# A two-layer decoder on one core: weights split during the experts, operands carried on chip into the second scan, and a rewritten last stage

## The reference

```python
x = _layernorm(x + ssm0(x));  x = _layernorm(x + long_conv(ctx, ctx, x))
x = _layernorm(x + moe0(x))       # 64 experts, the 8 best per token, 128 places each
x = _layernorm(x + ssm1(x));  x = _layernorm(x + linear_attention(x, ctx))
x = _layernorm(x + moe1(x))       # 4 experts, the 2 best per token, 512 tokens each

# moe0, the end: each token sums the outputs of its slots
slot_out = yb[dest] * topk_w.reshape(-1)[:, None]
out = jnp.zeros((T, h), yb.dtype).at[slot_token].add(slot_out)

# ssm1: d_inner 1024, 16 states, rank 128
xs, z = jnp.split(x @ W_in.T, 2, axis=-1)
u = silu(conv4(xs) + conv_b)               # over 4 tokens, channel by channel
dt_r, Bm, Cm = split(u @ W_x.T, [128, 16, 16])
dt = jax.nn.softplus(dt_r @ W_dt.T + b_dt)
A = -jnp.exp(A_log)
h_t = exp(dt_t * A) * h_(t-1) + dt_t * B_t * u_t
y_t = sum over the 16 states of h_t * C_t, + u_t * D
return (y * silu(z)) @ W_out.T
```

## Time and profile before

| what | value |
|---|---|
| median of 3 runs | 4858.97 us (4854.84 to 4861.33) |
| the profiled execution | 4852.57 us |
| its span, first to last instruction | 4850.8 us |
| PE busy | 3962.7 us, 82% |
| DVE busy | 2806.8 us, 58% |
| ACT busy | 1669.2 us, 34% |
| POOL busy | 1387.6 us, 29% |
| DMA | 556.5 MB, mean 115 GB/s |
| first experts | 2214 to 2581 us |
| joint projection | 2581 to 2972 us |
| second scan | 2972 to 3859 us |
| last stage | 4776.5 to 4850.8 us |

### The profile page before, as it was taken

One profiled execution on the slowest core, in us unless ns is written; L12 is line 12 of the kernel. 1 busy time (PEld: TensorE's weight loads), 2 busy tenths in 40 slices (PEclk: granted clock), 3 DMA queues, 4 the chain that ended last, 5 costly groups with the idle time before them and its releaser, 6 DMA issues. The chain is left out here.

```text
span 4850.8 us, 61695 instructions
## 1 busy us (share of the span) xinstructions
PE 3962.7 (82%) x19902; PEld 3073.2 (63%) x19902; DVE 2806.8 (58%) x4963; ACT 1669.2 (34%) x3411; POOL 1387.6 (29%) x1202
## 2 busy tenths in 40 slices
PE   7886799989999777867995994887778688849992
PEld 7886677767777565654454883665556466727772
DVE  5554344454443465983226875999999755533335
ACT  4343222223222120032222774555555422203431
POOL 0000000000000002754224533999999600010002
PEclk9998899999999888978997997999999899959996
DMA  3324333343333371117996535222222211123324
GB/s 108 131 87 140 98 84 90 89 109 85 89 85 89 76 249 66 44 37 261 317 317 197 178 123 205 83 83 83 83 90 83 80 56 50 45 58 119 104 95 122
DMA packets 532330, 556.51 MB, mean 115 GB/s; under 512 B 157795, under 2 KB 431523, under 8 KB 526544
## 3 DMA queue, kind: packets, MB, share of 16 engines
q1 hardware_dynamic: 497728, 470.19, 31.6%
q0 software_dynamic: 29632, 75.97, 4.7%
q10 hardware_dynamic: 4816, 8.53, 0.5%
HBM read 440.09 MB, written 135.43 MB: 119 GB/s over the span
## 5 line engine op out<-in xcount | busy, mean ns | idle before, releaser
L2333 PE MATMUL d_py<-d_h,d_ident 128*128 128x256 f32 x2048 | 530.1, 416 | 169.2 <-POOL d_h L2163 154.3
L2171 POOL TENSOR_TENSOR d_dBu<-d_B,d_dtu 128x1024 f32<-128x1024 f32 x256 | 597.0, 2364 | 118.0 <-DMA d_dt<-dt 118.0
L2333 PEld LDWEIGHTS d_py<-d_h,d_ident 128*128 128x128 f32 x2048 | 418.6, 209 | 276.8 <-POOL d_h L2163 182.8
L722 PE MATMUL a_pB<-a_uhi,a_whi 128*128 128x512 f32 x1152 | 495.0, 430 | 50.0 <-DVE a_ulo L609 44.3
L722 PE MATMUL a_pB<-a_uhi,a_wlo 128*128 128x512 f32 x1152 | 465.5, 404 | 0.0
L722 PE MATMUL a_pB<-a_ulo,a_whi 128*128 128x512 f32 x1152 | 464.7, 403 | 0.0
L2217 ACT ACTIVATE d_ph<-d_dt,d_A 128x255 f32<-128x255 f32 x1024 | 425.8, 461 | 0.1
L2277 DVE TENSOR_TENSOR_SCAN d_ph<-d_ph,d_dBu 128x1024 f32<-128x1024 f32 x160 | 365.9, 2287 | 24.4 <-ACT d_ph L2217 12.1
L1054 POOL TENSOR_TENSOR b_kv<-b_c 128x128 f32 (+11 forms) x256 | 100.3, 431 | 800.8 <-DMA b_c<-ctx_turned 796.2
L530 POOL DMA_DIRECT2D a_uraw<-u_feat x48 | 25.8, 539 | 1060.8 <-DVE a_ulo L609 621.2
L722 PEld LDWEIGHTS a_pB<-a_uhi,a_whi 128*128 128x128 f32 x1152 | 225.2, 195 | 118.0 <-DVE a_wlo L613 36.3
(11 more groups left out here) (481 smaller groups left out, 9453.3 us busy)
## 6 DMA issues: line engine op xcount, KB each, us to landing
c_gu<-w_gu SPq DMA_DIRECT2D x64, 768.0 KB, 5.5
a_wraw<-w_bc SPq DMA_DIRECT2D x48, 768.0 KB, 7.2
a_alall<-alpha SPq DMA_DIRECT2D x24, 1024.0 KB, 5.0
c_wd<-w_down SPq DMA_DIRECT2D x64, 256.0 KB, 6.5
slots_y<-c_y POOLq DMA_DIRECT2D x64, 256.0 KB, 7.3
f_w1r<-w SPq DMA_DIRECT2D x64, 256.0 KB, 2.8
f_w2r<-w SPq DMA_DIRECT2D x64, 256.0 KB, 2.9
d_B<-bc SPq DMA_DIRECT2D x7, 2048.0 KB
```

What stands on the lines that cost most here:

```text
L722: ins = nc.tensor.matmul(out, a[:, k, cols], b[:, k, ts], start=(k == 0 and n == 0), stop=(k == F - 1 and n == 2))
L2171: pool.tensor_tensor(dBu[c % RB][:, :, :], B_sb[i][:, q * G:(q + 1) * G, :], dtu_sb[i][:, f, :].unsqueeze(1).to_broadcast([P, G, L]), ALU. ...
L2333: ins = nc.tensor.matmul(py[f % 2][:, 0:L], ident_sb[:, :], h_sb[c % RH][:, n, :], start=False, stop=(q == Q - 1 and n == G - 1))
```

## The change

1. **Places and weights** of both routers are written straight into SBUF tensors that live on (`pl[:, at, :]`, `wk[:, at, :]`). The stores in the routers and the loads in the two stages that use them are gone.

2. **The split of w_in** moves into the rounds of the first experts. w_in is laid out so that a round's piece is one load of 512 KB.

```diff
@@ moe0_experts, SP, at the end of a round
+                sp.wait_ge(s_wl, r + 1)
+                alone(sp, tick_sp)
+                sp.dma_start(w_raw[:, :], w_in[bass.ds(r, 1), :, :].rearrange("a p n -> (a p) n")).then_inc(s_raw, 16)
@@ ACT, at the end of a round
+                act.wait_ge(s_raw, r * 16 + 16)
+                nc.scalar.copy(piece(w_hi, r), w_raw[:, :]).then_inc(s_wh, 1)
@@ DVE, at the end of a round
+                dve.wait_ge(s_wh, r + 1)
+                nc.vector.tensor_tensor(piece(w_lo, r), w_raw[:, :], piece(w_hi, r).bitcast(F32), ALU.subtract).then_inc(s_wl, 1)
```

```diff
@@ mix_project, SP
+            sp.wait_ge(s_pz, NB * F1)
+            sp.dma_start(carried.A[:, :, :], ...)
+            sp.dma_start(carried.D[:, :], ...)
             step_sizes(LAST - 1)
+            sp.wait_ge(s_out_dtu, 16)
+            sp.dma_start(carried.dtu[:, :, :], dtu_feat[:, :, 0:L]...)
+            sp.wait_ge(s_dts, 16)
+            sp.dma_start(carried.dt[:, :, :], dt_feat[:, :, 0:L]...)
             small(LAST)
-            step_sizes(LAST)
+            sp.wait_ge(s_out_u[0], 16)
+            sp.dma_start(carried.u[:, :, :], u_feat[:, :, 0:L]...)
+            for s, src, dst, stored in ((s_dt, r_last, dt_feat, s_dts), (s_dtu, v_last, dtu_feat, s_out_dtu)):
+                sp.wait_ge(s, LAST + 2)
+                sp.dma_start(dst[:, :, LAST * L:NB * L]..., src[:, :, :]).then_inc(stored, 16)
@@ POOL
+            for b in range(NB):
+                for c in range(2):
+                    for k in range(K_):
+                        if b == 0 and c == 0:
+                            pool.wait_ge(s_set, k + 1)
+                        else:
+                            pool.wait_ge(s_mix, (b * 2 + c - 1) * K_ + k + 1)
+                        pool.indirect_dma_start(g[k][:, :], None, y_slots, ...places[:, 2 * b + c, k:k + 1]...)
+            for f in range(F1):
+                pool.tensor_scalar(carried.skip[:, f, :], ident_sb[:, :], carried.D[:, f:f + 1], None, ALU.mult)
+            pool.tensor_scalar(carried.A[:, :, :], carried.A[:, :, :], -1.0, None, ALU.mult)
@@ ACT, the last batch
-                biased(LAST, f)
-            logs(LAST)
+                act.wait_ge(s_pd, LAST * F1 + f + 1)
+                nc.scalar.activation(v_last[:, f, :], pd[f % 2][:, 0:L], ACT.Abs, bias=bdt_sb[:, f:f + 1], scale=1.0)
+            link(nc.scalar.activation(v_last[:, :, :], v_last[:, :, :], ACT.Exp, scale=-1.0))
+            for h in HALVES:
+                nc.scalar.activation(v_last[:, h, :], v_last[:, h, :], ACT.Ln, bias=one_sb[:, :], scale=1.0)
+            nc.scalar.activation(carried.A[:, :, :], carried.A[:, :, :], ACT.Exp)
@@ DVE, the last batch
-            step_sizes(LAST, 1)
+            for f in range(F1):
+                nc.vector.tensor_scalar(r_last[:, f, :], pd[f % 2][:, 0:L], bdt_sb[:, f:f + 1], 0.0, ALU.add, ALU.max)
+            for n, h in enumerate(HALVES):
+                nc.vector.tensor_tensor(r_last[:, h, :], v_last[:, h, :], r_last[:, h, :], ALU.add)
+                nc.vector.tensor_tensor(v_last[:, h, :], r_last[:, h, :], u_sb[LAST % 2][:, h, :], ALU.mult)
```

6. **The last stage** is a new function, `mix_out`, in place of `gather_mix_norm`:

```diff
+            for n in range(TILES // PER):          # SP: x in four loads of 1 MB, at the start
+                sp.dma_start(x_sb[:, n * PER:(n + 1) * PER, :], ...).then_inc(s_x[n], 16)
+            for t in range(TILES):                 # SP stores a tile when it is ready
+                sp.wait_ge(s_ln, t + 1)
+                sp.dma_start(out[t * P:(t + 1) * P, :], o_sb[:, t, :]).then_inc(s_out, 16)
+            def root(t):                           # ACT
+                nc.scalar.activation(sd[:, t:t + 1], mv[:, t, 1:2], ACT.Sqrt, bias=eps_sb[:, :], scale=1.0)
+            def scaled(t):                         # ACT
+                nc.scalar.activation(o_sb[:, t, :], x_sb[:, t, :], ACT.Identity, bias=shift[:, t:t + 1], scale=sd[:, t:t + 1])
+            for t in range(TILES):                 # DVE, 6 gather buffers
+                mixed(t)
+                moments(t)
+                if t:
+                    shifted(t - 1)
```

More of the change, by code:

```diff
@@ L1 @@
+import math
 from contextlib import ExitStack
@@ L1117, with norm_route @@
 FAR = 1 << 20
-def norm_route(nc, v_sb, router, ident, before, ramp, tokens_of, x_tok, slot_token, places, weights):
+def norm_route(nc, v_sb, router, ident, before, ramp, tokens_of, x_tok, slot_token, pl, wk):
     LN_EPS = 1e-5
@@ L1637, with __init__, cut @@
 DI1, N1 = 1024, 16
 F1 = DI1 // P
-class FirstBC:
-    def __init__(self, nc, phase):
+class Carried:
+    def __init__(self, nc, phase, place, end):
         m = Space(nc, "d0", phase)
         self.B, self.C = m.sb("B0", [P, N1, L]), m.sb("C0", [P, N1, L])
-        self.loaded = m.sem("ldB0")
-def mix_project(nc, first_bc, y_slots, x_in, places, weights, ident, w_in, conv_w, conv_b, w_x, w_dt, b_dt, x_tok, u_feat, z_feat, dt_feat, dtu_feat, bc_feat):
+        at = [place]
+        def cut(name, *shape):
+            start, at[0] = at[0], at[0] + 4 * math.prod(shape)
+            return nc.alloc_sbuf_tensor_at("d0_" + name, [P, *shape], F32, offset=start)
+        self.dtu, self.dt, self.u, self.z = (cut(n, F1, L) for n in ("dtu", "dt", "u", "z"))
+        self.wo, self.skip, self.A, self.D = cut("wo", F1, D), cut("skip", F1, P), cut("A", F1, N1), cut("D", F1)
+        assert at[0] <= end
+        self.loaded, self.streams, self.u_in = m.sem("ldB0"), m.sem("ldstreams0"), m.sem("ldu0")
+        self.raw, self.exped, self.ready = m.sem("ldA"), m.sem("expA"), m.sem("ready")
@@ L1653, in mix_project @@
+def mix_project(nc, carried, y_slots, x_in, places, weights, ident, w_hi, w_lo, conv_w, conv_b, w_x, w_dt, b_dt, a_log, skip, x_tok, u_feat, z_feat, dt_feat, dtu_feat, bc_feat):
     LAST = NB - 1
@@ L1668, in mix_project @@
         xm = [m.sb(f"xm{i}", [P, 2, D]) for i in range(2)]
-        pl = [m.sb(f"pl{i}", [P, 2, K_], U32) for i in range(2)]
         wk = [m.sb(f"wk{i}", [P, 2, K_]) for i in range(2)]
@@ L1802, in parts @@
                     nc.scalar.copy(x_hi[i][:, :, c * P:(c + 1) * P], po[c][:, :].rearrange("p (k t) -> p k t", k=KD)).then_inc(s_xh, 1)
-            def chunk(n):
-                k, cols = CHUNKS[n]
-                act.wait_ge(s_w[n], 16)
-                nc.scalar.copy(w_hi[:, k, cols], w_raw[n]).then_inc(s_wh, 1)
-            for n in range(len(CHUNKS)):
-                chunk(n)
             root(0)
@@ L1828, in project @@
             def project(b, r, i):
+                if isinstance(b, int) and b == LAST - 1:
+                    act.wait_ge(s_out, 16)
+                    for dst, at in ((carried.B, 0), (carried.C, N1 * L)):
+                        act.dma_start(dst[:, :, :].rearrange("p n t -> p (n t)"), bc_feat[0, at:at + N1 * L].partition_broadcast(P)).then_inc(carried.loaded, 16)
                 for f in range(F1 + 1):
@@ L1871, in _, with weights_of @@
             nc.vector.memset(eps_sb[:, :], LN_EPS).then_inc(s_set, 1)
-            dve.sem_inc(s_mix, K_)
-            for k in range(K_):
-                nc.vector.memset(g[k][:, :], 0.0).then_inc(s_set, 1)
             dve.wait_ge(s_set, 4 + K_)
+            def weights_of(b, i):
+                nc.vector.tensor_copy(wk[i][:, :, :], weights[:, bass.ds(2 * b, 2), :]).then_inc(s_wk, 1)
+                dve.wait_ge(s_wk, b + 1)
             def mixed(b, n, i):
@@ L2152, in spread_ready, with streams_ready @@
         def spread_ready(eng, k, i):
-            eng.wait_ge(first_bc.loaded, 32)
+            eng.wait_ge(carried.loaded, 32)
             if i or not first(k):
                 eng.wait_ge(s_B[i], (k + i) * 32)
+        def streams_ready(eng, k, i):
+            eng.wait_ge(carried.streams, 32)
+            if i or not first(k):
+                eng.wait_ge(s_dt[i], (k + i) * 32)
         @block.gpsimd
@@ L2324, in batch @@
                         if f == 0:
-                            pe.wait_ge(s_u[i], k * 16 + 16)
+                            pe.wait_ge(carried.u_in, 16)
+                            if i or not first(k):
+                                pe.wait_ge(s_u[i], (k + i) * 16)
                         pe.wait_ge(s_yz, reached(b, f, F1, 1))
@@ L2651, with moe1_route @@
 FAR = 1 << 20
-def moe1_route(nc, x_feat, w_router, b_router, before, ramp, tokens_of, ident, digits, digits_int, row_token, places, weights):
+def moe1_route(nc, x_feat, w_router, b_router, before, ramp, tokens_of, ident, digits, digits_int, row_token, pl, wk):
     ROUNDS, TRIALS = 10, 7
@@ L2697, in moe1_route @@
         s_lane, s_at, s_at_pool, s_named, s_tab = (m.sem(n) for n in "lane at at_pool named tab".split())
-        s_const, s_lv, s_loop, s_log, s_d, s_e, s_count, s_total, s_taken, s_before, s_pl, s_out = (
-            m.sem(n) for n in "const lv loop log d e count total taken before pl out".split())
+        s_const, s_lv, s_loop, s_log, s_d, s_e, s_count, s_total, s_taken, s_before, s_pl = (
+            m.sem(n) for n in "const lv loop log d e count total taken before pl".split())
```

368 lines of the change are left out of this document (163 added, 205 removed).

## The result

The changed kernel takes 4798.88 us (median of 4 runs, 4796.18 to 4801.57) against 4858.60 for the kernel before on the same chip: a ratio of 0.9879, 95% interval 0.9863 to 0.9895, 59.7 us less. 4801 was predicted. A second comparison, on another occasion, gave 4797.80 against 4855.09 and 0.9883 (0.9867 to 0.9900).

The account below looks back on a forecast made before the run. PE bounds the experts; at five other places it idles, waiting for loads. Terms +1.2 - 14.3 - 11.8 - 14.1 - 3.5 - 15.3 = -57.8 from 4852.57 give 4794.8; the median lies 6.4 higher: 4801 us, range 4789 to 4819.

Parts of the forecast that it names:

- The +1.2: Experts: the 1.22 us subtract on DVE exceeds its slack ahead of PE at some round boundaries, costing 1.2 us.
- the edge at 338 GB/s: Experts: 328 GB/s at a share of 0.97 gives 338 at full share; the change asks for 340 in the fullest round.
- from the last mix to px 6.4: Joint projection's start: time from the last mix's start to the first px stays 6.4 us, within a term of -14.3.
- The step that named the buffers as what removes the wait: Joint projection's end: with z and u buffers instead of v and r, the last batch's first bias starts 11.8 us earlier.
- The 1.0 for the backlog: Joint projection's end: about 5 MB of loads queue from 2930 on, with remaining stores behind; 1.0 us put on that.
- The pace of 2.9: Last stage: DVE bounds at 2.9 us per tile, down from 3.83; the stage takes 59.0 us, 15.3 less.
- Rival D: Last stage: DVE's order is tighter than 2.9 and gathers pace, 6 us less: 4795; chance 0.09.
- Rival B: Starts of joint projection and last stage: memsets beside gathers hold up descriptor writing, total 4809; chance 0.13.
- the recorded sign of it: Joint projection's start: first px above 34 us into the stage would show its gathers taking over 1.3 us.
- C: Experts become DMA-bound, every new byte paid, 12 us more: 4814; chance 0.12.
- E: Second scan's start: carried operands are not on chip, 10 of the 14.1 us come back: 4812; chance 0.06.
- F: Joint projection's loop: gathers in a row for seven batches bound it, 102 us more, 4903, slower than before; chance 0.01.

Follow-up runs that it names:

- the second pair: Second profiles of both unchanged versions, the kernel before and the changed kernel; the second scan took 889.13 us before and 873.93 us changed.
- Before again: The kernel before, unchanged, run for a second profile; first experts 367.16 us, joint projection 389.74 us, last stage 76.02 us.
- the early Sqrt: Changed kernel plus a 128x1 Sqrt on ACT at the joint projection's start, run alongside other edits; first px 33.22 and 32.73 us into the stage.
- the second load: Changed kernel with each round's piece of w_in loaded twice, the second into an unused buffer (4.19 MB more); experts' stage 368.40 us.

## Why the prediction came out

The sum was 57.8 us, the medians say 59.7 and 57.3. Term by term, from the first pair of profiles:

| term | predicted | measured |
|---|---|---|
| experts | +1.2 | +0.8 |
| joint projection, start | -14.3 | -11.9 |
| its loop | 0 | +1.1 |
| its end | -11.8 | -10.8 (-11.6 to the bias, +0.8 behind it) |
| second scan | -14.1 | -12.7 (-15.2 in the second pair) |
| routers | -3.5 | -3.6 at the second's end |
| last stage | -15.3 | -17.5 |

The measured column adds up to 54.6 us less. The second pair, read the same way, gives 56.0. The spans of the two pairs differ by 53.5 and 63.3, so the code that the change leaves alone adds up to +1.1 us in one pair and to -7.3 in the other. So the sum was right within 2 to 3 us, and that the median came out within 3 us of 4801 is in part luck.

**Experts: no bound by DMA, as said; the size not shown.** The +1.2 took the slacks of one execution. Before again has 2.10, 1.81, 1.85, 1.90, 2.10, 1.29 and 1.65 us at the same seven boundaries, none below the 1.22 of the subtract, and by the same step would have given nothing. In the changed kernel PE waited 0.17 and 0.53 us for c_h; the rest of the +0.8 is elsewhere, and the stage took 366.9 to 369.2 in the eleven profiles with one subtract. With two, the step said 6 and 2.4 were measured. The step that put the edge at 338 GB/s was wrong too, and so was its sentence that no row showed more: a round of the kernel before moved 353 GB/s, and 362 was reached without harm. The Trainium skill's 358 (DMA: Bandwidth & Descriptors, Where 436 GB/s comes from) was nearer than a rate scaled up by a busy share; it too was passed, if by 1%.

**Start of the joint projection: mechanism right, 2.4 too much.** The step "from the last mix to px 6.4" failed: it was 7.9, since before, ACT loaded the root's table while it waited for work, and now it does so behind the moments (1.28; the early Sqrt gave it back). The first gather came at 1.48, not 0.9, and the gathers' pace was 1.38, not 1.3, which makes 1.2 us over fifteen: four of the sixteen began while a sum ran on DVE and took 1.27 to 1.50 us (last section). The landing was better than taken (3.9 for 4.7).

**End: size right, cause half wrong.** The step that named the buffers as what removes the wait was the failure. The same buffers with early B and C kept 7 of the 11.6 us, so the wait was as much a queue as a buffer, and I should have read how long the store took to land (13.3 us for 1 MB) before crediting the buffer. Behind the bias three small terms were put wrong or for the wrong reason. The last multiply ended 0.5 and not 1.0 earlier by the halves (Ln's start to its end 6.12, before 6.65). The biases took 0.4 us more (8.53 for 8.14; 8.01 for 7.50 in the second pair), which 7.2 to 8.5 over the changed kernels with two banks hardly tells from scatter. The 1.0 for the backlog is there between the last store and the next stage (7.69, before 6.65), but not as a backlog: without the carried loads it stayed at 7.66. The rows point to the pair of stores. From the store of the last dt to the next stage it is 8.97 and 8.98 us in the two profiles before and 8.91 to 8.94 in all changed kernels but the one with B and C late; the store of dtu behind it is only issued sooner, 1.25 us after it in place of 2.33. By this what counts is when dt's store is issued, and the halves made that 0.5 us later, since a multiply now stands between the two adds. No run with the add and multiply whole has tested it.

**Scan: right**, mechanism and size (12.7 and 15.2 for 14.1); the streams alone carry 9 us of it.

**Last stage: mechanism right, 2.2 too little.** The pace of 2.9 came from a mean over 16 tiles, 3.83, that has the turns of the hardware loop in it; inside its body the tiles followed each other in 3.60, and 3.60 - 0.55 - 0.36 = 2.69 would have been the 2.66 that was measured. The prediction's sum had 2.9 x 15 and so 3.6 us too much there; the first sum (9.19 for 8.5) and the end (7.7 for 7.0) took 1.4 of that back. Rival D had the first half of this and wrongly saw the gathers take over. The tiles inside one turn of the old loop, their first two sums in one row each:

```profile
4790.26 1.52 DVE L1615 SCALAR_TENSOR_TENSOR f_x<-f_g,f_wk,f_x 128x512 f32<-128x512 f32 x2
4793.86 1.53 DVE L1615 SCALAR_TENSOR_TENSOR f_x<-f_g,f_wk,f_x 128x512 f32<-128x512 f32 x2
```

**The rest.** Rival B is refuted for memsets by the gathers beside none, and the change of 8 us that it stood for did not come. But its reason, that DVE holds up a gather, is real with the sums in the memsets' place, and the recorded sign of it (first px above 34, gathers over 1.3) was about met: 33.96 and 34.30, with gathers at 1.38 and 1.40. C is refuted by the second load, E by POOL's start at 0.11; F's loop lost 1.1 us and not 100. In the twelve changed profiles the loop took 306.1 to 308.2 us against 305.8 and 305.9, so a small loss is real; the profile with B and C issued later had the shortest, which one run does not prove. The two largest misses, 2.4 us too much at the start and 2.2 too little in the last stage, cancel, and a part of the closeness is that too.

## What to carry to other kernels

When two parts of a change could each remove the same wait, the gain belongs to neither alone: look at how long the transfer that ends the wait takes to land, and at what was queued ahead of it. Take the pace of an unrolled loop from neighbours inside the old loop's body, not from a mean over its turns, and a slack from more than one execution. A wait that ends a stage hides small things of other engines, here a table load and an exchange of two banks; they are next on the path once it is gone.
